# A gated cross-attention and mixture-of-experts kernel: the head written out as a function of its own on each engine

## What is computed

```
n1  = layernorm(x)
p   = softmax((n1 Wq^T)(ctx Wk^T)^T / sqrt(128))
x   = x + tanh(g_xattn) * p (ctx Wv^T)
h   = layernorm(x)
logits = h/|h| @ sim/|sim| - sigmoid(gates)      # 16 experts for each token
w   = softmax over the experts whose relu(logit) > 0 (the top 2 where none is)
q,k,v = sum over e of w[:, e] * (h @ proj[e])    # for q_proj, k_proj and v_proj
o   = softmax(q k^T / sqrt(128)) v
x   = x + tanh(g_ffn) * sum over e of w[:, e] * (o @ o_proj[e])
```

## Time and profile before

| what | us |
|---|---|
| median of 3 runs | 849.62 (849.38 to 850.53) |
| the profiled execution, its own time | 849.49 |
| its span in the profile | 847.7 |
| PE busy | 808.5 (95%) |
| DVE busy | 563.0 (66%) |
| ACT busy | 442.0 (52%) |
| POOL busy | 484.1 (57%) |

### The profile page before, as it was taken

One profiled execution on the slowest core, in us unless ns is written; L12 is line 12 of the kernel. 1 busy time (PEld: TensorE's weight loads), 2 busy tenths in 40 slices (PEclk: granted clock), 3 DMA queues, 4 the chain that ended last, 5 costly groups with the idle time before them and its releaser, 6 DMA issues.

```text
span 847.7 us, 13843 instructions
## 1 busy us (share of the span) xinstructions
PE 808.5 (95%) x4280; PEld 451.3 (53%) x4280; DVE 563.0 (66%) x1944; ACT 442.0 (52%) x1148; POOL 484.1 (57%) x701
## 2 busy tenths in 40 slices
PE   3479999999999999999999999999999999999996
PEld 3345555555555555555555555555555555554442
DVE  2767475757587575758757575875757586575647
ACT  3555646456454645646464564646456464544433
POOL 2266656564665656466565646666564665655524
PEclk9569999999999999999999999999999999999998
DMA  8753332041323214142421414242151423214000
GB/s 219 210 200 96 113 109 100 22 162 45 139 76 121 100 35 153 43 139 75 122 98 44 147 39 139 75 123 98 28 164 39 140 75 116 98 50 139 26 12 26
DMA packets 40138, 83.85 MB, mean 99 GB/s; under 512 B 3520, under 2 KB 20096, under 8 KB 40064
## 3 DMA queue, kind: packets, MB, share of 16 engines
q1 hardware_dynamic: 39344, 82.88, 30.2%
q10 hardware_dynamic: 720, 0.08, 0.1%
HBM read 78.23 MB, written 4.72 MB: 98 GB/s over the span
## 4 chain that ended last, share of the span: by engine, by line
PE 90%; DVE 4%; POOL 2%; ACT 2%; issue 1%; DMA 1%; ACTq 0%; DVEq 0%; POOLq 0%
PE acc_v L938 19%; PE acc_k L938 19%; PE acc_q L938 19%; PE y L950 9%; PE oT_p L950 9%; PE oT_p L1076 2%; PE m L1012 2%; PE m L1003 2%; PE m L1107 1%; PE m L1095 1%; DVE x_all L806 1%; PE m L1067 1%; PE m L1042 1%; PE m L995 1%; PE m L1047 1%
## 5 line engine op out<-in xcount | busy, mean ns | idle before, releaser
L465 POOL TENSOR_TENSOR zq<-zq_full,zq 128x512 f16<-128x512 f32 x256 | 296.1, 1165 | 289.7 <-ACT zq L530 289.4
L530 ACT ACTIVATE zq<-zq_full 128x512 f16<-128x512 f32 x256 | 160.9, 640 | 223.8 <-DVE zq_full L778 222.4
L938 PE MATMUL acc_q<-zq,w_hi 128*128 128x512 f16 x512 | 194.8, 381 | 0.0
L938 PE MATMUL acc_k<-zq,w_hi 128*128 128x512 f16 x512 | 194.5, 380 | 0.0
L938 PE MATMUL acc_v<-zq,w_hi 128*128 128x512 f16 x512 | 194.5, 380 | 0.0
L806 DVE SCALAR_TENSOR_TENSOR x_all<-y,w_out,x_all 128x128 f32<-128x128 f32 x356 | 122.1, 343 | 93.3 <-issue 82.2
L778 DVE TENSOR_TENSOR zq_full<-wq_bc,x2T_p 128x512 f32<-128x512 f32 x256 | 166.6, 674 | 2.0 <-ACT x2T_p L635 1.5
L806 DVE SCALAR_TENSOR_TENSOR x_all<-oT_p,w_out,x_all 128x128 f32<-128x128 f32 x356 | 121.5, 341 | 0.0
L479 POOL TENSOR_TENSOR x_all<-y_sc,x_all 128x128 f32<-128x128 f32 x240 | 100.4, 454 | 20.0 <-DVE x_all L806 13.2
L938 PE MATMUL acc_q<-zq,w_lo 128*128 128x512 f16 x256 | 97.5, 381 | 0.0
L938 PE MATMUL acc_v<-zq,w_lo 128*128 128x512 f16 x256 | 97.2, 380 | 0.0
(11 more groups left out here) (175 smaller groups left out, 1136.7 us busy)
## 6 DMA issues: line engine op xcount, KB each, us to landing
wq_bc<-w_rows SPq DMA_DIRECT2D x128, 512.0 KB, 4.1
out_dram<-x_all SPq DMA_DIRECT2D x16, 256.0 KB, 6.6
ctx_g<-in_ctx_dram SPq DMA_DIRECT2D x16, 154.0 KB
x_all<-in_x_dram SPq DMA_DIRECT2D x2, 256.0 KB, 6.6
x_all<-in_x_dram SPq DMA_DIRECT2D x1, 512.0 KB, 9.2
w_rows<-wT SPq DMA_DIRECT2D x16, 32.0 KB, 1.8
wq_sb<-in_L_xattn_Wq_dram SPq DMA_DIRECT2D x1, 64.0 KB, 5.2
wk_sb<-in_L_xattn_Wk_dram SPq DMA_DIRECT2D x1, 64.0 KB, 6.1
```

What stands on the lines that cost most here:

```text
L465: nc.gpsimd.tensor_tensor(zq[:, 1, e % Z_SLOTS, :], zq_full[:, e % F_SLOTS, :], zq[:, 0, e % Z_SLOTS, :], ALU.subtract).then_inc(zq_lo_poo ...
L530: nc.scalar.activation(zq[:, 0, e % Z_SLOTS, :], zq_full[:, e % F_SLOTS, :], ACT.Copy).then_inc(zq_hi_done, 1)
L938: last = nc.tensor.matmul(acc[m][:], w[:, m, s, :], zq[:, half, s % Z_SLOTS, :], start=(s == 0 and n == 0), stop=(s == E - 1 and n == 2))
```

## The change

The head becomes a function `head()` on each engine that is called once, and `passes` runs from i = 0. The order of the head is written out by hand, and the pieces of the bodies that head and body share become functions.

- SP: the projections are issued after wq and wk have landed; then the second context, k, v, x(1), o, x(2) and the third context. The last three parts of x are issued in passes 0, 1 and 2 at s=5.
- PE: the transposes of the context and the product of wk and wq come first, then the values' part and the statistics of sim_matrix. The transposes of group 1's normed x go to acc[Q] instead of m0.
- ACT: the constants (sigmoid, tanh, exp) are evaluated behind xnT_out(0).
- The maxima are shared in two turns: q, k and v in the head (turn 0), o in pass 0 (maximum at s=2, transpose and product at the end of s=4 and s=6, DVE's steps at s=5 and s=7). The high part of o is made at s=9, the low part at s=11.
- The chain that normalises sim_matrix (`setup_gate`) is behind the scales instead of ahead of them.
- POOL: first_rstd(1) comes ahead of the first four zq, first_rstd(2) behind them; on DVE first_stats(2) is the last step of the head.

```diff
...
-        HIGH_AT = [(-1, 2), (-1, 4), (-1, 8), (0, 1)]
-        LOW_AT = [(-1, 7), (-1, 9), (-1, 10), (0, 3)]
+        MAX_AT, SHARE_AT = (0, 2), ((0, 4), (0, 6))
+        HIGH_AT = (0, 9)
+        LOW_AT = (0, 11)
...
-            for m, w in enumerate((q_proj, k_proj, v_proj, o_proj)):
+            def load_weights(m, w):
                 sp.dma_start(stage[:, m], w.rearrange("e c h -> c e h")).then_inc(proj_in[m], 16)
-                if m == 0:
-                    load_x(1)
-            for c in range(2, len(X_LOADS) - 1):
-                load_x(c)
...
+            def head():
+                sp.wait_ge(kq_in, 16 * 2)
+                load_weights(Q, q_proj)
+                load_context(1)
+                load_weights(K, k_proj)
+                load_weights(V, v_proj)
+                load_x(1)
+                load_weights(O, o_proj)
+                load_x(2)
+                load_context(2)
+                weight_rows(0)
+                for j in range(W_SLOTS):
+                    spread_q(0, j)
+                for j in (4, 5):
+                    spread_q(0, j)
...
+                    if s == 5 and i + 3 < len(X_LOADS) - 1:
+                        load_x(i + 3)
...
+            def head():
+                first_rstd(0)
+                setup_norms()
+                second_rstd(0)
+                second_norm(0)
+                first_rstd(1)
+                for e in range(LEAD):
+                    zq_low(0, e)
+                first_rstd(2)
...
+            def constants():
+                act.wait_ge(small_in, 16 * 5)
+                nc.scalar.activation(sig[:], gates_b[:], ACT.Sigmoid)
+                nc.scalar.activation(tanh_x[:], gx[:], ACT.Tanh)
+                nc.scalar.activation(tanh_f[:], gf[:], ACT.Tanh).then_inc(tanh_done, 1)
+                act.wait_ge(tanh_done, 1)
+                act.wait_ge(prep_pe, 2)
+                nc.scalar.activation(wvT[:], acc[K][:, 0:P], ACT.Copy, scale=tanh_x[:]).then_inc(wvT_done, 1)
+                nc.scalar.activation(exp_0[:], tanh_f[:], ACT.Exp)
...
-                act.wait_ge(prep_dve, 5)
+                act.wait_ge(scales_done, 1 if m < O else 2)
...
+            def head():
+                ctxT_out(0)
+                act.wait_ge(prep_pe, 1)
+                nc.scalar.activation(m_kq[:], acc[Q][:, 0:P], ACT.Copy).then_inc(m_kq_done, 1)
+                x_norm(0)
+                kxT_out(0)
+                xnT_out(0)
+                constants()
+                x_exps(0)
+                vx_out(0)
+                pxT_out(0)
+                x2_norm(0)
+                x2T_out(0)
+                weight_high(Q)
+                ctxT_out(1)
+                x_norm(1)
+                gate_exps(0)
+                kxT_out(1)
+                xnT_out(1)
+                weight_high(K)
+                wT_out(0)
+                weight_high(V)
+                x2T_move(0)
+                x_exps(1)
+                vx_out(1)
+                pxT_out(1)
+                for e in range(LEAD):
+                    zq_high(0, e)
...
+                    if (i, s) == HIGH_AT:
+                        weight_high(O)
...
+            SHARE_BANKS = ((acc[V], acc[K]), (y0, oT_p))
+            SHARE_STEPS = 6
+            def share_largest(turn):
+                dve.wait_ge(wmax_ps, 2 * turn + 1)
+                nc.vector.tensor_reduce(wmax_t[:], SHARE_BANKS[turn][0][0:4, 0:P], AX_X,
+                                        ALU.max).then_inc(share_step, 1)
+                dve.wait_ge(share_step, SHARE_STEPS * turn + 1)
+                nc.vector.tensor_scalar(wmax_d[:], ident[0:4, 0:4], wmax_t[:], None, ALU.mult).then_inc(share_step, 1)
+            def weight_scales(turn):
+                step = SHARE_STEPS * turn
+                cols = slice(Q, O) if turn == 0 else slice(O, O + 1)
+                dve.wait_ge(wmax_ps, 2 * turn + 2)
+                nc.vector.tensor_scalar(wmax_all[:, cols], SHARE_BANKS[turn][1][:, cols], 2.0 ** -60, 2.0 ** 60,
+                                        ALU.max, ALU.min).then_inc(share_step, 1)
+                dve.wait_ge(share_step, step + 3)
+                nc.vector.tensor_scalar(w_pow[:, cols].bitcast(U32), wmax_all[:, cols].bitcast(U32), 0x7F800000, None,
+                                        ALU.bitwise_and).then_inc(share_step, 1)
+                dve.wait_ge(share_step, step + 4)
+                nc.vector.reciprocal(w_up[:, cols], w_pow[:, cols]).then_inc(share_step, 1)
+                if turn == 0:
+                    nc.vector.tensor_scalar(score_scale[:], w_pow[:, Q:Q + 1], w_pow[:, K:K + 1], RSQRT_C,
+                                            ALU.mult, ALU.mult).then_inc(share_step, 1)
+                else:
+                    nc.vector.tensor_scalar(out_scale[:], w_pow[:, V:V + 1], w_pow[:, O:O + 1], 1.0 / W_UP,
+                                            ALU.mult, ALU.mult).then_inc(share_step, 1)
+                dve.wait_ge(share_step, step + 6)
+                nc.vector.tensor_scalar(w_up[:, cols], w_up[:, cols], W_UP, None, ALU.mult).then_inc(scales_done, 1)
+                if turn == 1:
+                    dve.wait_ge(tanh_done, 1)
+                    nc.vector.tensor_scalar(out_scale[:], out_scale[:], tanh_f[:], None, ALU.mult).then_inc(scales_done, 1)
...
+                dve.wait_ge(scales_done, 3)
...
+            def head():
+                first_stats(0)
+                setup()
+                x_max(0)
+                weight_max(Q)
+                x_sum(0)
+                weight_max(K)
+                x1_add(0)
+                second_stats(0)
+                weight_max(V)
+                share_largest(0)
+                weight_scales(0)
+                setup_gate()
+                first_stats(1)
+                x2_norm_inverse(0)
+                gate_logits(0)
+                gate_mask(0)
+                gate_softmax(0)
+                weight_low(Q)
+                x_max(1)
+                weight_low(K)
+                weight_low(V)
+                x_sum(1)
+                zq_scale(0, 0)
+                zq_scale(0, 1)
+                x1_add(1)
+                zq_scale(0, 2)
+                zq_scale(0, 3)
+                second_stats(1)
+                first_stats(2)
...
+                    if (i, s) == MAX_AT:
                         weight_max(O)
-                        setup_weights()
-                    if (i, s) in LOW_AT:
-                        weight_low(LOW_AT.index((i, s)))
+                    if (i, s - 1) == SHARE_AT[0]:
+                        share_largest(1)
+                    if (i, s - 1) == SHARE_AT[1]:
+                        weight_scales(1)
+                    if (i, s) == LOW_AT:
+                        weight_low(O)
...
+            def setup_queries():
+                pe.wait_ge(kq_in, 16 * 2)
+                nc.tensor.matmul(acc[Q][:, 0:P], wk_sb[:], wq_sb[:], start=True, stop=True).then_inc(prep_pe, 1)
+            def setup_values():
+                pe.wait_ge(small_in, 16 * 5)
+                nc.tensor.transpose(acc[K][:, 0:P], wv_sb[:], ident[:]).then_inc(prep_pe, 1)
+                pe.wait_ge(prep_dve, 1)
+                nc.tensor.matmul(acc[V][:, 0:E], ones[:], sim_sq[:], start=True, stop=True).then_inc(prep_pe, 1)
+            def gather_max(turn, bank):
+                pe.wait_ge(wmax_done, 3 + turn)
                 pe.wait_ge(prep_dve, 3)
-                nc.tensor.transpose(acc[V][0:4, 0:P], wmax[:], ident[:]).then_inc(wmax_ps, 1)
-                pe.wait_ge(prep_chain, 4)
+                nc.tensor.transpose(bank[0:4, 0:P], wmax[:], ident[:]).then_inc(wmax_ps, 1)
+            def spread_max(turn, bank):
+                pe.wait_ge(share_step, 6 * turn + 2)
                 pe.wait_ge(wvT_done, 1)
-                nc.tensor.matmul(acc[K][:, 0:4], ones[0:4, :], wmax_d[:], start=True, stop=True).then_inc(wmax_ps, 1)
+                nc.tensor.matmul(bank[:, 0:4], ones[0:4, :], wmax_d[:], start=True, stop=True).then_inc(wmax_ps, 1)
...
-                    pe.wait_ge(wmax_ps, 2)
-                    pe.wait_ge(prep_chain, 5)
+                    pe.wait_ge(share_step, 3)
+                    pe.wait_ge(xnT_sb, 2)
...
+            def head():
+                pe.wait_ge(consts, 1)
+                ctx_transpose(0)
+                setup_queries()
+                setup_values()
+                pe.wait_ge(m_kq_done, 1)
+                kx_product(0)
+                xn_transpose(0)
+                for b in range(G):
+                    small_product(-2, 9, b)
+                pe.wait_ge(wvT_done, 1)
+                vx_product(0)
+                px_transpose(0)
+                att_product(0)
+                gather_max(0, acc[V])
+                x2_transpose(0)
+                spread_max(0, acc[K])
+                pe.wait_ge(prep_dve, 4)
+                for b in range(G):
+                    small_product(-1, 4, b)
+                ctx_transpose(1)
+                kx_product(1)
```

(34 more changed lines are left out.)

342 lines of the change are left out of this document (156 added, 186 removed).

## The result

The changed kernel takes 845.99 us (median of 5 runs, 845.81 to 846.13); the kernel before, on the same chip, 849.95 us. The ratio is 0.9953, 95% interval 0.9939 to 0.9968: 4.0 us faster, with 845.99 beside the 846.2 forecast. The span of the profiled execution went from 847.7 to 844.0, so 3.7 us are there to be found.

A forecast was written before the change was run, and what follows sets the result against it. TensorE, busy 95% of the span, bounds the kernel, so only its waits in the 53 us head could be won. 6.2 - 2.4 - 0.4 = 3.4 us off 849.49, plus 0.13 to the median, gives 846.2; range 843.8 to 849.6.

The forecast's parts named there:

- Part 1: Start to first softmax: small matrices first and constants later bring x's first scores to DVE near 15.0, gain 3.9 us.
- Part 2: Head's loads: q waits for wk, k lands at 18.2, statistics end at 22.9 instead of 27.30, gain 4.4 us.
- Rival (b): Head bound by its loads, or table loads on DVE's path; T at 49 to 50, 848 to 849 us; chance 0.10.
- Part 3: Scales, gate and splits in the head: scales gain 2.9 us, gate 3.6; T at 47.0, 6.2 us gained.
- T: End of the head's last product on TensorE: 53.21 in the kernel before, forecast at 47.0.
- Part 4: First pass: first_rstd(2) ahead of second_rstd(1) on GpSimd delays x2; TensorE waits 2.4 us before its transposes.
- give-back: Part of the head's gain lost in the first pass while TensorE waits for x2, forecast at 2.4 us.
- Rival (a): No wait in the first pass, so most of the 6.2 us stays: 843.4 to 844.5 us; chance 0.10.
- Rest of the pass: First pass: moving out's maximum and split costs a net 0.4 us (bounds: 0.3 gained, 1.0 lost).
- (d): Clock kept low in the first pass, rising only behind its second wait: 854.8 us; chance 0.05.
- (e): Head ends as late as before because DMA or DVE fills the same time: 849.5 us; chance 0.03.
- Rival (c): Clock falls in the first pass's wait for x2; 6.6 us at half speed cost 3.3: 849.5 us; chance 0.10.

The follow-up runs named there:

- e2: Changed kernel without SyncE's wait for wq and wk ahead of q, so q is issued at once: 846.68 us, ratio 0.9964 to the kernel before.
- e9: Changed kernel with group 2's statistics and inverse deviation behind second_rstd(1), plus 34 extra products in TensorE's idle stretches of the head: 844.05 us.
- e1: Changed kernel with first_stats(2) on DVE and first_rstd(2) on POOL moved from the head into pass 0, the latter behind second_rstd(1): 844.67 us.
- e11: Changed kernel with the last three loads of x issued back in the head, behind load_x(2), instead of in passes 0 to 2: 845.86 us.
- e5: Changed kernel with the product that spreads o's maximum at slot 7 of pass 0 instead of slot 6: 845.80 us; profiled execution 846.44.
- e3: Changed kernel with the constants (sigmoid, tanh, exp) back at the front of ScalarE's head: 847.10 us, ratio 0.9967 to the kernel before.
- e7: Changed kernel with first_rstd(2) behind second_rstd(1), o's maximum spread a slot later and wT ahead of k's high part, together: 844.86 us.
- e4: Changed kernel with o's maximum and scale back in the head, all four scales shared in one turn: 847.46 us, ratio 0.9977 to the kernel before.
- e8: Changed kernel with 34 extra 128x128 float32 products that nothing needs, placed where TensorE waits in the head: 845.01 us.
- e12: The changed kernel itself measured again, nothing altered: 845.90 us, ratio 0.9958 to the kernel before.
- e6: Changed kernel with wT_out(0) ahead of the high part of k on ScalarE: 847.33 us, ratio 0.9976 to the kernel before.
- e10: Changed kernel with o's maximum spread one slot later and 7 extra 128x128 products directly before x2's transposes in pass 0: 845.70 us.

## Why the prediction was right

By its steps, measured in the changed kernel:

- **Part 1.** Product of wk 7.28 (in brackets what was taken: 8.26), first maximum of x 13.80 (15.0), softmax 15.25 (16.3), its product ends at 20.52 (20.2). The gain up to the maximum is 5.05 us, not 3.9: the small matrices land a microsecond sooner when q isn't beside them (e2). The forecast had this, at half the size, only as a bound of k's landing. What was gained was lost again by 20.5, because the last two products ran at 1.2 GHz: 1.14 and 2.08 us, where the 3.9 us taken from the kernel before hold 0.66 and 1.16. The second table load is exposed (13.85 to 15.13) and costs nothing, since DVE is waiting for k; but k's maximum (to 20.6) and the product (to 20.5) end together, so nothing is spare.
- **Part 2.** k is there at 18.33 (18.2), statistics end at 23.01 (22.9), the largest of v ends at 25.17 (25.1). These came true by two errors of 1.0 us that cancel: q was issued at 7.32 and not at 8.3, and took 6.7 us to land (at 14.0) and not 5.7. The 1 us in it for the last bytes is shown by no row by itself. Rival (b) falls: DVE waits for k 1.55 us, for v not at all.
- **Part 3.** x2 ends at 26.70 (26.6), scales from 28.42, the up scale at 29.30 (29.3), w_new ends at 36.23 (36.3), splits at 43.64 (44.1), wT at 38.34 (39.1), rows issued at 40.47 (41.0), first broadcast used at 44.98 (44.3 to 45.5). T is 46.18 (47.0). The mis-sized term is wT: ACT did the high part of k right after xnT, at 36.45.
- **First expert.** It was said to start with T. It started 1.54 us behind T, at 47.72, when its low part was ready; forecast for that was 47.3. The prediction's "starts with T" failed because T came sooner and the rows did not. It cost nothing, since x2 was awaited behind it; in e9 it is the bound.
- **Part 4.** x2's transposes at T+10.5 (T+10.4), by the queue order on GpSimd. From T, first_stats(2) ends at +4.7 (4.7), first_rstd(2) at +6.8 (6.75), second_rstd(1) at +8.8 (8.7), x2 at +10.5 (10.4). The wait before the transposes was 1.67 and not 2.4, because TensorE arrived 0.8 us later than T+8.0, having started 1.5 later. What counts, the give-back from T+8.0, was 2.5 (2.4). Rival (a) falls; e1 shows what it would have been: 844.7.
- **Rest of the pass.** 0.8 us lost (0.4). The wait for the spread maximum is 0.86, about 0.4 was taken; no other gap above 0.6 us is in the first pass. No wait for the high and low parts of o, the memset, the second bank or the x loads is among the gaps (for the x loads e11 tests it).
- **Rivals (d) and (e)** fall with the same rows: the clock is up from 50.5, ahead of both waits, and T is 7.0 earlier.
- **Sum.** 7.0 − 2.5 − 0.8 = 3.7 against 6.2 − 2.4 − 0.4 = 3.4. The gain of T was put 0.8 too low, give-back and pass 0.5 too cheap; the two errors cancel all but 0.3.

**Rival (c), the argument that failed.** The prediction set the clock's fall aside because from 10 to 15 us TensorE was busy 1.75 of 5 us and "kept full speed", by the record of the granted clock. That reading was wrong. The timeline of PE of the kernel before:

```profile
12.65 1.11 PE L1053 MATMUL m<-ident,xn 128*128 128x128 f32 x4 [3.08 <-ACT xn L589]
...
36.28 1.12 PE L1053 MATMUL m<-ident,xn 128*128 128x128 f32 x4 [1.47 <-ACT xn L589]
```

The same four transposes take 1.11 us at 12.65, where the record says 1.00, and 1.12 at 36.28, where it says 0.50; at full clock they take 0.60 (61.20 in the earlier trace rows). Until about 20.5 the kernel before ran at 1.2 GHz too; the transposes at 20.75 are its first of full-clock length (0.66). In the changed kernel the record says 1.00 for the whole head while its products have the lengths of 1.2 GHz. The busy time by stretch of the changed kernel:

```profile
30.00:40.00 10.00, 8.58 (x33) 6.71 (x34) 8.73 (x39) 7.91 (x12) 1.69 (x4) 1.00 0.08 20
```

The timeline of PE of the changed kernel, within that stretch:

```profile
34.80 1.11 PE L1179 MATMUL acc_q<-ident,xn 128*128 128x128 f32 x4 [0.48 <-ACT xn L595]
```

So nothing in the rows spoke against (c), and its chance should have been higher. Its price was too high: 1.7 us (e5) and not 3.3, since the clock was low for 3.3 us of work, from 57.5 to 60.8, and not for 6.6. That the clock stayed up was luck: the wait came out at 1.67 us because expert 0 started late, and not at the 2.4 of the forecast, which lies above every wait in the table below that left the clock up and above four that did not. Over the runs, TensorE's longer waits at full clock ended in two ways (those for the spread maximum, 1.09 at most, left the clock up as well):

| wait, us | where | clock behind it |
|---|---|---|
| 0.59, 0.70, 1.09, 1.18 | x2 in e3, e2, e7, e4 | stays |
| 1.22 | expert 0 in e8 | stays |
| 1.52, 1.57, 1.67 | x2 in e11, e12, changed kernel | stays |
| 1.94, 1.94 | x2 in e5, expert 0 in e9 | falls |
| 1.98, 1.99 | group 1's xn in the head of e8, of e9 | falls, in e9 already within the wait |
| 2.98, 3.83 | x2 in e8, e6 | falls |

That is one profiled execution of each; where exactly the border lies, and whether it lies at the same place in each execution, they do not show. Only the association is shown: e10, meant to test the cause, missed it.

## What to carry to other kernels

When work is moved earlier, look for the step of a later group that an in-order engine now does ahead of the one awaited: here it made TensorE wait 1.67 us of the 7.0 that the head had gained, and two moved calls brought 1.3 us back. Large loads that nothing asks for yet can wait for the small ones ahead of them: here it brought the first steps a microsecond. Read the clock from the lengths of equal products, not from its record alone, and price an idle TensorE of two microseconds as the wait plus what the clock takes behind it.

## What the hardware showed that was not expected

- The record of the granted clock says 1.00 until its first change, whatever the clock is: 1.11 us for four 128x128 transposes at a recorded 1.00, 0.60 at a true one.
- The clock fell behind idle stretches as short as 1.94 us (also 1.98 and 1.99), and in e5 that cost 1.7 us, nearly as long as the wait itself. All seven waits between 0.59 and 1.57 us and one of 1.67 left it up.
- When it rises is not fixed by the work. From the start of expert 0, after which TensorE has no gap, it took 1.9 us (e6, where expert 0 follows the head's last product with no wait), 2.8 (changed kernel), 3.2 (e11), 3.3 (e5, e7), 3.7 (e4), 3.8 (e12), 5.1 (e1), 5.3 (e3), 5.5 (e2) and 5.8 (e10). The changed kernel and e12 are one program; e10 and the changed kernel start expert 0 at the same time. Two programs alike up to that point differ by 3.0 us. The Trainium skill calls this moment "run-variable" (TensorE: Matmul & The Clock Gate, What's actually happening), and the trace agrees; the half microsecond that the page gives for it (What you observe) is too small for these runs, and the measurement decides. At half speed that is 1.5 us of work; a wait behind it hides it, as in the changed kernel, and without one it shows in the time. It is as large as most effects measured here.
- Products of 128x128 in f32 that nothing needs brought TensorE to 2.4 GHz in the head (0.66 against 1.12 us for the transposes), where the head's own work, busy for 8.58 of 10 us from 30 to 40, had not. They did not hold it there: it fell at 34.9 in e8 and at 33.7 in e9, and was back at 41.7 and 40.5.
- GpSimd's first instruction on 128x4 values took 0.23 us where no split ran beside it (51.03), against 2.23 in the earlier trace rows, as the rule that the prediction cites has it.
